# The work between the stages of a graph network kernel: loads, factors, a spill tile and a norm put elsewhere

## The chip, the cores and the metric

The kernel runs on one core of a Trainium2 chip. A core has TensorE (PE, matmuls), VectorE (DVE), ScalarE (ACT), GpSimd (POOL) and SyncE (SP, which only issues DMAs here). They run their own instruction streams and meet at semaphores. The metric is the device time of one execution in microseconds.

## The reference

12,500 nodes with 64 features, and 412,500 edges (200,000 random pairs in both directions and a loop for each node), sorted by destination. Three attention layers, then a mean-like graph convolution, each with a residual and a layer norm:

```python
x = features; out = features
for l in range(3):
    f1 = relu(x[row] @ nb_W[l] + nb_b[l]);  f2 = relu(x[col] @ self_W[l] + self_b[l])
    h = relu(concat([f1, f2]) @ att1_W[l] + att1_b[l])
    mask = clip(sigmoid(h @ att2_W[l] + att2_b[l]) * 1.5 - 0.45, 0, 1)
    d = clip((segment_sum(mask, row) + 1e-6) ** -0.5, 0, 10)
    x = segment_sum(mask * d[row] * d[col] * x[col], row)
    out = out + x
x = layernorm(features + out)
g = degree ** -0.5
h = relu(segment_sum(g[row] * g[col] * x[col], row) @ weight + bias)
return layernorm(x + h)
```

## The kernel before

**Blocks and tiles.** Nodes lie 128 to a block, in NB = 98 blocks of rows. The kernel first sorts the edges on chip and places those of a block of rows in TT = 50 tiles of 128 slots, in NG = 7 groups of 7 or 8 tiles (`GROUPS`, one PSUM bank each, `z_banks`). 49 tiles belong to pairs of column blocks; the 50th takes edges that did not fit, gathered by index (`xg`). What fits nowhere goes to "slow" spill tiles; with these inputs there is one of them (`n_slow` = 1), and `over_slow` loops over it. One-hot matrices for a block of rows (`oct`, `ort`, `orr`; 2.4 MB) are made in layer 0, kept in DRAM (`one_hots`) and loaded again in every later stage, in three pieces (`PIECES`).

**Stages.** Each of the layers 0 to 2 has a node stage (`node_stage`, `nodes_of`: two 64-wide products for each node, tables `q_table` and `p_planes` in DRAM), a score stage (`edges_of`: `cols` and `rows` matmuls, `hidden` and `logits` on DVE, a sigmoid on ACT, `masks`, `row_sums` into `rs`), a node factor `dinv` from `rs`, a scaled table (`scaled_table`: x times `dinv`, cut into three bf16 planes `tab` by `planes_of`, and stored as `xd_table` for the gathers) and a stage of sums (`segment_sums`). After layer 2 come a norm, a fourth scaled table and a fourth stage of sums with all masks 1, a last product and the last norm.

**A block in the stage of sums.** `cols` on PE picks the table rows of the 7 groups into PSUM. For each group DVE multiplies by the mask (`weighted`, L1828), ACT writes the high bf16 part back to PSUM (L908), DVE subtracts it (`rest`, L1835), POOL subtracts the next part (`low_planes`, L740), and PE adds all parts up by destination (`scatter`, L1180). DVE's order is `weighted` 0, `weighted` 1, `rest` 0, `weighted` 2, `rest` 1, and so on, with `sums` of the block before (L1840) behind `weighted` 3. POOL's order is the gather of the 50th tile (L670), groups 0 to 3, that tile's product (L728), groups 4 to 6. `z_ps`, `z_used`, `high_ps`, `low_ready`, `sc_ps` count these hand-overs. `over_rows` writes block 0 out and loops over the other 97.

**Between the stages.** SP issues in program order: the spill tile's loads, the store of the spill mask and a wait for it, a wait for all rows of the table, the table store (L623, 3136 KB in one DMA), then the one-hot loads of the stage (L500). POOL starts the stage when the store has landed. After the sums DVE adds the spill tile to `x_cur` (L1868), multiplies `x_cur` by `dinv` (L1901), and copies the next layer's weights (L1445, L1446), for which PE, ACT and POOL wait. POOL adds `x_cur` to `total` in the next score stage (L719). After layer 2 DVE adds it (L1913), and the norm is a row of passes over all 6272 columns: L1918 sum, L1922 subtract, L1924 square, L1926 sum, L1934 multiply; then the factor of the convolution, a memset of all masks (L1946), and the table.

Of the kernel before, what the change touches and what calls it, by code (L numbers as in the profile page):

```python
# [50 lines left out]
def gnn_kernel(nc, x, src, dst, nb_W, nb_b, self_W, self_b, att1_W, att1_b, att2_W, att2_b,  # L51
# [35 lines left out]
    TURNS_LATE = 12  # L87
    ROUNDS = -(-(E // S + NB) // XP)
# [15 lines left out]
    with ExitStack() as ctx:  # L104
# [255 lines left out]
        s_out = sem("slow_out")  # L360
        out_ready = sem("out_ready")
# [72 lines left out]
        def _(sp):  # L434
            sp.sem_inc(xd_out, 16)
# [104 lines left out]
            def edge_loads(layer):  # L540
# [22 lines left out]
                over_rows(sp, layer * (2 * NB), layer * NB, block_of_rows)  # L563
                rows_again(sp.snap(layer * NB + NB - 1), NB - 1)

            def segment_loads(t0, layer):
                def block_of_rows(t, m, R, late):
                    if not late:
                        wait_alone(sp, z_ps, t * NG + NG)
                        wait_alone(sp, sc_ps, m * NG + NG)  # L570
                        for i in range(3):
                            load_oct(R, i)
                        if not (isinstance(layer, int) and layer == L):
                            wait_alone(sp, rs_ps, layer * NB + NB + 1)
                        load_or(R, 0)
                        return
# [18 lines left out]
            def slow_loads(layer, first, edges):  # L595
                def tile(q, at, b):
# [8 lines left out]
                    if edges:  # L605
                        sp.dma_start(s_ix[:, 1, :], fields(sprow_d)).then_inc(s_in, 16)
                        wait_alone(sp, s_v, q * SLOW_V + 1 + SLOW_MASK)
                        sp.dma_start(smask_d[row, :].rearrange("o (p j) -> (o p) j", j=XS), s_mask).then_inc(s_out, 16)
                        wait_alone(sp, s_out, layer * n_slow * 16 + at * 16 + 16)
                    else:  # L610
                        sp.dma_start(s_mask, smask_d[row, :].rearrange("o (p j) -> (o p) j", j=XS)).then_inc(s_in, 16)
                over_slow(sp, n_slow, first, tile)

            def layer(l, first):
# [4 lines left out]
                else:  # L619
                    edge_loads(l)  # L620
# [1372 lines left out]
```

## Time and profile before

| | |
|---|---|
| median of 3 runs | 9728.46 us (9728.18 to 9734.29) |
| profiled execution | 9734.98 us, its span 9733.3 us |
| DVE, PE busy | 7868.9 us, 7865.2 us (81% each) |
| POOL, ACT busy | 3627.5 us, 3111.2 us |
| score stage of layer 1 | 4156 to 5326 us |
| sums of layer 0, 1, 2 | 3131 to 4050, 5378 to 6302, 7633 to 8555 us |
| sums of the convolution | 8654 to 9575 us |

The profile times every instruction of one execution, in microseconds from the span's start. The busy time of an engine is a share over stages that have different limits, so it is read stage by stage. Where an operation follows another of its engine at once, the two overlap a little, and the distance of the starts is what one costs.

### The profile page before, as it was taken

To read this page: it belongs to the slowest core of one execution; us is meant where nothing else is said; L and a number is where in the kernel's file an instruction comes from. 1 tells how busy PE (TensorE), PEld (TensorE's weight loads), DVE (VectorE), ACT (ScalarE), POOL (GpSimd) and SP (SyncE) were. 2 spreads that over 40 slices of the span, in tenths; PEclk is the share of its full clock that TensorE was granted. 3 is DMA by queue.
4 is the path that set the end of the run, shared out by engine and by line. 5 is a ranking of instruction groups with operands and counts; after the bars stand their busy time and mean duration, and the time that the engine had idled before them with its cause. 6 is when DMAs were issued, how large, how long until landed. Compare 5 with 4: busy or idle time off the path is not lost. (4 is left out here: it accounts for less than half of the span.)

```text
span 9733.3 us, 754656 instructions
## 1 busy us (share of the span) xinstructions
PE 7865.2 (81%) x306604; PEld 7523.1 (77%) x306604; DVE 7868.9 (81%) x13926; ACT 3111.2 (32%) x6110; POOL 3627.5 (37%) x4194
## 2 busy tenths in 40 slices
PE   0112239999997999989998899989999799959996
PEld 0012138888886999888997899879989799959995
DVE  9998169999997888877777788877777788878885
ACT  0010026666665444410001344320000344424442
POOL 0001510000001888510000788710000588848882
PEclk9755568999898999999999999999999899979996
DMA  1000137777775666567776666567777566646662
GB/s 28 0 0 11 33 94 241 240 240 239 241 241 179 178 178 178 141 198 209 206 208 179 170 179 178 155 174 207 209 207 207 152 178 177 178 113 178 178 177 71
DMA packets 983353, 1593.44 MB, mean 164 GB/s; under 512 B 249463, under 2 KB 732603, under 8 KB 982879
## 3 DMA queue, kind: packets, MB, share of 16 engines
q1 hardware_dynamic: 954104, 1563.61, 55.0%
q0 software_dynamic: 29152, 28.55, 1.7%
q8 instruction: 60, 0.98, 0.0%
q14 instruction: 37, 0.30, 0.0%
HBM read 1308.71 MB, written 283.01 MB: 164 GB/s over the span
## 5 line engine op out<-in xcount | busy, mean ns | idle before, releaser
L1053 PE MATMUL bank<-tab,extra 128*64 128x64 bf16 x201684 | 3599.9, 197 | 469.3 <-DMA extra<-one_hots 229.7
L1053 PEld LDWEIGHTS bank<-tab,extra 128*64 128x64 fp8e4 x201684 | 3478.8, 113 | 582.7 <-issue 555.7
L740 POOL TENSOR_TENSOR planes<-planes 128x448 f32<-128x448 f32 (+1 forms) x2744 | 2598.4, 950 | 540.0 <-DVE planes L1835 471.5
L908 ACT CAST bank<-planes 128x448 f32<-128x448 bf16 (+1 forms) x2744 | 1471.7, 545 | 1848.9 <-DVE planes L1828 1848.9
L1828 DVE TENSOR_TENSOR planes<-bank,mask_all 128x448 f32<-128x448 f32 (+2 forms) x2744 | 1665.9, 619 | 331.1 <-PE bank L1053 247.7
L1835 DVE TENSOR_TENSOR planes<-planes,bank 128x448 f32<-128x448 f32 (+1 forms) x2744 | 1707.6, 622 | 220.3 <-ACT bank L908 125.6
L1180 PE MATMUL bank<-planes,extra 128*64 128x192 bf16 x39200 | 1840.5, 248 | 16.5 <-issue 4.3
L1180 PEld LDWEIGHTS bank<-planes,extra 128*64 128x64 fp8e4 x39200 | 1685.6, 108 | 61.4 <-issue 11.1
L670 POOL DMA_INDIRECT xg<-q_table,ixb x294 | 279.0, 949 | 3761.2 <-ACT ixb L838 2204.7
L1708 DVE SCALAR_TENSOR_TENSOR extra<-bank,a2w 128x448 f32<-128x448 f32 (+1 forms) x2058 | 1263.6, 629 | 449.6 <-PE bank L1076 412.3
L1076 PE MATMUL bank<-plb,extra 128*128 128x64 bf16 x44100 | 1520.5, 196 | 10.7 <-issue 3.1
L1076 PEld LDWEIGHTS bank<-plb,extra 128*128 128x128 fp8e4 x44100 | 1424.0, 100 | 22.5 <-issue 10.3
L1715 DVE TENSOR_REDUCE lg<-extra 128x7 f32<-128x448 f32 (+1 forms) x2058 | 1232.4, 619 | 0.0
L869 ACT CAST extra<-bank 128x512 fp8e4<-128x512 f32 (+2 forms) x1470 | 717.3, 516 | 483.4 <-PE bank L1088 467.7
L1724 DVE TENSOR_SCALAR extra<-work,iota_p 128x2816 fp8e4<-128x2816 uint8 (+2 forms) x490 | 644.2, 1349 | 63.9 <-issue 30.6
L873 ACT COPY plb<-planes 128x192 bf16 (+1 forms) x294 | 103.8, 353 | 1607.0 <-PE bank L1076 1605.4
L970 PE MATMUL bank<-ident,tab 128*128 128x128 f32 x224 | 40.6, 366 | 676.1 <-DVE tab L1335 676.1
L970 PEld LDWEIGHTS bank<-ident,tab 128*128 128x128 f32 x224 | 39.0, 198 | 678.2 <-issue 344.2
L1088 PE MATMUL bank<-total,extra 128*128 128x128 bf16 x4900 | 511.5, 238 | 61.9 <-DVE rs L1696 42.7
L670 POOL DMA_INDIRECT xg<-xd_table,ixb x392 | 385.0, 982 | 315.4 <-issue 175.9
L1101 PE MATMUL bank<-mk,extra 128*128 128x4 bf16 x14700 | 410.3, 164 | 25.9 <-DVE mk L1692 14.4
L1101 PEld LDWEIGHTS bank<-mk,extra 128*128 128x128 fp8e4 x14700 | 392.1, 95 | 46.3 <-issue 33.9
(245 smaller groups left out, 4283.8 us busy)
## 6 DMA issues: line engine op xcount, KB each, us to landing
extra<-one_hots SPq DMA_DIRECT2D x1372, 352.0 KB, 3.1
extra<-one_hots SPq DMA_DIRECT2D x2156, 224.0 KB
extra<-one_hots SPq DMA_DIRECT2D x588, 208.0 KB
one_hots<-extra SPq DMA_DIRECT2D x490, 224.0 KB, 4.7
one_hots<-extra SPq DMA_DIRECT2D x294, 352.0 KB, 3.2
work<-slot_rows_cols SPq DMA_DIRECT2D x196, 352.0 KB, 4.9
work<-slot_rows_cols SPq DMA_DIRECT2D x294, 224.0 KB, 4.9
work<-slot_rows_cols SPq DMA_DIRECT2D x98, 208.0 KB
```

The lines of the kernel that those rows point to most:

```text
L670: nc.gpsimd.indirect_dma_start(out=to, out_offset=None, in_=table_d, in_offset=bass.IndirectOffsetOnAxis(ap=index, axis=0)).then_inc(done, 16)
L740: nc.gpsimd.tensor_tensor(tiles(yrl[:, 2, a * C:b * C]), tiles(yrl[:, 1, a * C:b * C]), upper[:, 1, a:b, :], ALU.subtract).then_inc(low_re ...
L869: nc.scalar.copy(orr[:, k * P:(k + n) * P], turn_to(j)[:, 0:n * P], saturate=False).then_inc(or_made, 1)
L908: nc.scalar.copy(tiles(z_banks[g][:, 0:(b - a) * C]), upper[:, 0, a:b, :]).then_inc(high_ps, 1)
L1053: mm = pe.matmul(bank[half * S:(half + 1) * S, i * C:(i + 1) * C], oct_[:, k * P + half * S:k * P + (half + 1) * S], tab[:, at:at + C], st ...
L1076: mm = pe.matmul(bank[:, i * C:(i + 1) * C], ort[:, k * P:(k + 1) * P], plb[:, pl * C:(pl + 1) * C], start=False, stop=True, skip_group_ch ...
L1101: mm = pe.matmul(sum_bank[:, 0:NPL + 1], orr[:, k * P:(k + 1) * P], mk_upper[:, k, :], start=(k == 0), stop=(k == TT - 1), skip_group_chec ...
L1180: mm = pe.matmul(sum_bank[lo:lo + S, 0:NPL * C], orr[:, k * P + lo:k * P + lo + S], upper[:, :, k, :], start=(k == 0), stop=(k == TT - 1))
L1708: v.scalar_tensor_tensor(tiles(yv[g % 3][:, 0:w]), tiles(bank_of(g, first)[:, 0:w]), 0.0, a2w[:].unsqueeze(1).to_broadcast([P, w // C, C]) ...
L1715: v.tensor_reduce(lg[:, k0:k1], tiles(yv[g % 3][:, 0:(k1 - k0) * C]), AX_X, ALU.add).then_inc(lg_done, 1)
L1828: v.tensor_tensor(tiles(yrl[:, 0, a * C:at * C]), tiles(z_banks[g][:, 0:(at - a) * C]), mask_all[:, bass.ds(R * TT + a, at - a)].unsqueeze ...
L1835: v.tensor_tensor(yrl[:, 1, a * C:b * C], yrl[:, 0, a * C:b * C], z_banks[g][:, 0:(b - a) * C], ALU.subtract).then_inc(z_used, 1)
```

## The change

1. `first_segment_loads`: SP issues the one-hot loads of the stage of sums ahead of the table store, which goes out in 7 parts (`scaled_rows_out`), each when its rows are scaled. `xd_out` counts the parts.
2. `scale`: the factor `dinv` and the addition to `total` are applied to the block before, in each turn of `segment_sums` of layers 0 to 2, behind `weighted` 5 and ahead of `rest` 4. The product over all of `x_cur`, POOL's additions to `total` and the last one on DVE are gone. The spill tile is added with its factor to both.
3. In layers 1 and 2 the spill tile of the score stage is worked on first on DVE and POOL, and behind block 0 on PE, ACT and SP (`behind_first`). Its matmul goes to `sum_bank`, `rs` begins as zeros, and `sums` adds to it. ACT issues the store of its mask.
4. The next layer's weights are copied behind block 0 of the sums, and ACT's sigmoid table is loaded there.
5. The norm after layer 2: no separate pass for squares on DVE (ACT squares parts while DVE subtracts and sums in turns), the two factors are joined into one for the table, POOL writes the normed x and the masks of ones.

```diff
-        def over_rows(eng, t0, n0, body):
+        def over_rows(eng, t0, n0, body, behind_first=None):
             body(value(eng, t0), value(eng, n0), 0, False)
+            if behind_first is not None:
+                behind_first()
...
+            def first_segment_loads(t0, layer):
+                wait_alone(sp, z_ps, value(sp, t0 * NG + NG))
+                wait_alone(sp, sc_ps, value(sp, layer * NB * NG + NG))
+                for i in range(3):
+                    load_oct(0, i)
+                if not (isinstance(layer, int) and layer == L):
+                    wait_alone(sp, rs_ps, value(sp, layer * NB + NB + 1))
+                load_or(0, 0)
+
+            def scaled_rows_out(k):
+                for i, (a, b) in enumerate(PARTS):
+                    wait_alone(sp, rows_ready, value(sp, k * NG + i + 1))
+                    sp.dma_start(table(xd_d)[:, a // C:b // C, :], w3[:, a // C:b // C, :]).then_inc(xd_out, 16)
...
-                        wait_alone(sp, s_v, q * SLOW_V + 1 + SLOW_MASK)
-                        sp.dma_start(smask_d[row, :].rearrange("o (p j) -> (o p) j", j=XS), s_mask).then_inc(s_out, 16)
-                        wait_alone(sp, s_out, layer * n_slow * 16 + at * 16 + 16)
...
-                slow_loads(l, l * 2, True)
-                wait_alone(sp, rows_ready, l * (2 * NG) + 2 * NG)
-                sp.dma_start(table(xd_d), w3).then_inc(xd_out, 16)
+                    edge_loads(l, lambda: slow_loads(l, l * 2, True))
...
+                first_segment_loads(l * (2 * NB) + NB, l)
+                scaled_rows_out(l * 2 + 1)
                 segment_loads(l * (2 * NB) + NB, l)
...
-                    if not late and not first:
-                        nc.gpsimd.tensor_tensor(total[:], total[:], x_cur[:], ALU.add).then_inc(total_added, 1)
...
+            wait_alone(pool, x_done, L * NB)
+            nc.gpsimd.memset(mask_all[:], 1.0).then_inc(ones_masks, 1)
+            pool.wait_ge(ones_masks, 1)
+            pool.wait_ge(norm_ready, 1)
+            for a, b in PARTS:
+                nc.gpsimd.tensor_tensor(x_cur[:, a:b].rearrange(view, c=C), total[:, a:b].rearrange(view, c=C),
+                                        nodeA[:, a // C:b // C].unsqueeze(2).to_broadcast([P, (b - a) // C, C]),
+                                        ALU.mult).then_inc(x_normed, 1)
...
+            def sigmoid_table(l):
+                wait_alone(act, layer_w, value(act, l + 1))
+                nc.scalar.activation(warm[:], a2b[:], ACT.Sigmoid)
...
+            for i, (a, b) in enumerate(PARTS):
+                wait_alone(act, centered, i + 1)
+                nc.scalar.activation(x_cur[:, a:b], total[:, a:b], ACT.Square).then_inc(part_squared, 1)
...
+                    edges_of(l, first, lambda: slow_edges(l, sum_bank))
...
+                def scale(t, R):
+
+                    rows, factor = bass.ds(value(dve, R * C), C), dinv[:, bass.ds(R, 1)]
+                    wait_alone(dve, or_done, t + 2)
+                    v.scalar_tensor_tensor(total[:, rows], to[:, rows], factor, total[:, rows], ALU.mult, ALU.add)
+                    v.tensor_scalar(to[:, rows], to[:, rows], factor, None, ALU.mult).then_inc(x_done, 1)
+
                 def block_of_rows(t, m, R, late):
                     for g in range(NG):
                         weighted(t, m, R, g)
                         if g == 3 and late:
                             sums(value(dve, m - 1), value(dve, R - 1))
+                        if g == 5 and late and scaled:
+                            scale(value(dve, t - 1), value(dve, R - 1))
                         if g:
                             rest(m, g - 1)
...
-                ns.done(v.tensor_tensor(x3, x3, per_node(dinv[:]), ALU.mult))
...
+            for i in range(NG + 2):
+                if i < NG:
+                    a, b = PARTS[i]
+                    rows = t3[:, a // C:b // C, :]
+                    v.tensor_tensor(rows, rows, dinv[:, a // C:b // C].unsqueeze(2).to_broadcast([P, (b - a) // C, C]),
+                                    ALU.subtract).then_inc(centered, 1)
+                if i >= 2:
+                    a, b = PARTS[i - 2]
+                    wait_alone(dve, part_squared, i - 1)
+                    ns.done(v.tensor_reduce(nodeA[:, a // C:b // C], x3[:, a // C:b // C, :], AX_X, ALU.add))
...
+            ns.done(v.tensor_tensor(g_both, nodeA[:], dinv[:], ALU.mult))
             ns.wait(dve)
-            scaled_table(2 * L)
-            segment_sums(L * 2 * NB, L, total)
+            scaled_table(2 * L, total, g_both)
+            dve.wait_ge(ones_masks, 1)
+            dve.wait_ge(x_normed, NG)
+            segment_sums(L * 2 * NB, L, total, False)
```

## Rows read from the trace of the kernel before

**Rows 1.** The page, busy us of each engine, share of the span, instructions.
```profile
PE 7865.2 (81%) x306604; PEld 7523.1 (77%) x306604; DVE 7868.9 (81%) x13926; ACT 3111.2 (32%) x6110; POOL 3627.5 (37%) x4194
```

**Rows 2.** Busy us in a stretch of layer 0's sums, PE clock, DMA share, GB/s.
```profile
3140.00:4035.00 895.00, 889.54 (x37800) 880.30 (x37795) 777.59 (x1436) 377.39 (x766) 747.71 (x860) 1.00 0.65 177
```

**Rows 3.** Waits in the same stretch: us in total, times, longest us.
```profile
DVE planes L1828 <- PE bank L1053: 39.9, 100, 2.3
```

**Rows 4.** Timeline of DVE in one block: start us, us, line, idle time before.
```profile
3605.13 0.61 DVE L1835 TENSOR_TENSOR planes<-planes,bank 128x448 f32<-128x448 f32 x1
3606.07 0.62 DVE L1828 TENSOR_TENSOR planes<-bank,mask_all 128x448 f32<-128x448 f32 x1 [0.33 <-PE bank L1053]
3606.62 0.35 DVE L1840 TENSOR_REDUCE x_cur<-bank 128x192 f32 x1
3606.88 0.61 DVE L1835 TENSOR_TENSOR planes<-planes,bank 128x448 f32<-128x448 f32 x1
...
3608.47 0.62 DVE L1828 TENSOR_TENSOR planes<-bank,mask_all 128x448 f32<-128x448 f32 x1
3609.01 0.61 DVE L1835 TENSOR_TENSOR planes<-planes,bank 128x448 f32<-128x448 f32 x1
```

**Rows 5.** Timeline of POOL in the same block.
```profile
3607.63 1.99 POOL L740 TENSOR_TENSOR planes<-planes 128x448 f32<-128x448 f32 x2 [0.81 <-DVE planes L1835]
3609.59 0.29 POOL L728 TENSOR_TENSOR planes<-xg,mask_all 128x64 f32<-128x64 f32 x1
```

**Rows 6.** Timeline of the first blocks of score stages 1 and 2.
```profile
4154.05 13.50 POOL L719 TENSOR_TENSOR total<-total,x_cur 128x6272 f32<-128x6272 f32 x1
...
4165.47 2.15 DVE L1685 TENSOR_SCALAR st_m<-sg 128x50 f32<-128x50 f32 x1 [0.55 <-ACT sg L843]
...
6408.32 13.48 POOL L719 TENSOR_TENSOR total<-total,x_cur 128x6272 f32<-128x6272 f32 x1
...
6419.99 1.86 DVE L1685 TENSOR_SCALAR st_m<-sg 128x50 f32<-128x50 f32 x1 [0.54 <-ACT sg L843]
```

**Rows 7.** Groups by line, DVE in the sort: count, busy us, mean ns.
```profile
L1335 DVE TENSOR_SCALAR tab<-tab,signs 128x4096 f32<-128x4096 f32 x7 | 16.5, 2353 | 0.3
```

**Rows 8.** Line L1685 in all layers: ns min, median, max.
```profile
L1685 DVE TENSOR_SCALAR st_m<-sg x294: 177/190/2149, 1412.7 to 7582.0; 128x50 f32<-128x50 f32 x147
```

**Rows 9.** Timeline where the sums of layer 0 and of the convolution start.
```profile
3111.31 0.39 SPq L623 DMA_DIRECT2D xd_table<-work  x1
...
3114.03 2.06 DVE L1435 TENSOR_TENSOR tab<-planes,tab 128x896 bf16<-128x896 f32 x2
...
3128.66 0.95 POOL L670 DMA_INDIRECT xg<-xd_table,ixb  x1 [44.14 <-DMA xd_table<-work]
...
3130.76 0.69 DVE L1828 TENSOR_TENSOR planes<-bank,mask_all 128x512 f32<-128x512 f32 x1 [14.68 <-PE bank L1053]
...
8653.72 0.69 DVE L1828 TENSOR_TENSOR planes<-bank,mask_all 128x512 f32<-128x512 f32 x1 [15.09 <-PE bank L1053]
```

**Rows 10.** Timeline between layer 0 and layer 1.
```profile
4055.32 0.22 DVE L1868 TENSOR_TENSOR x_cur<-x_cur,bank 128x64 f32 x1 [1.24 <-PE bank L1204]
...
4064.17 0.56 POOL L763 COPY extra<-x_cur 128x448 f32 x1 [12.48 <-DVE a2b L1446]
```

**Rows 11.** Timeline of the norm behind layer 2.
```profile
8560.22 0.22 DVE L1868 TENSOR_TENSOR x_cur<-x_cur,bank 128x64 f32 x1 [1.49 <-PE bank L1204]
...
8574.73 6.69 DVE L1918 TENSOR_REDUCE nodeA<-total 128x98 f32<-128x6272 f32 x1
...
8617.07 2.23 DVE L1677 TENSOR_TENSOR work<-x_cur,dinv 128x1024 f32<-128x1024 f32 x2
```

**Rows 12.** Timeline of DVE, first and last of score stage 1.
```profile
4156.76 1.42 DVE L1708 SCALAR_TENSOR_TENSOR extra<-bank,a2w 128x512 f32<-128x512 f32 x2 [3.76 <-PE bank L1076]
...
5332.25 0.16 DVE L1696 COPY rs<-bank 128x4 f32<-128x4 f32 x1 [4.44 <-PE bank L1101]
...
5337.87 0.46 DVE L1885 TENSOR_REDUCE dinv<-rs 128x98 f32<-128x294 f32 x1 [0.20 <-DVE rs L1816]
```

More of the change, by code:

```diff
@@ L568, in block_of_rows @@
                     if not late:
[L569 to L575, printed above, removed]
                         return
@@ L593, in segment_loads, with slow_loads @@
                     load_or(NB - 1, i)
-            def slow_loads(layer, first, edges):
+            def slow_loads(masks_of, first, edges):
                 def tile(q, at, b):
@@ L838, in indices, with sigmoids @@
                 nc.scalar.copy(ixb[:], colx[:, bass.ds(R * XT, XT)]).then_inc(ix_ready, 1)
-            def sigmoids(layer, first):
+            def sigmoids(layer, first, behind_first):
                 def sigmoid(n):
@@ L1056, in cols, with edges_of @@
                 return mm
-            def edges_of(layer, first):
+            def edges_of(layer, first, behind_first):
                 def cols_of(t, g):
@@ L1501, in _ @@
             layer_weights(0)
+            dve.wait_ge(layer_w, 1)
+            dve.wait_ge(xd_out, XD)
             nodes_of(0, True, range(0, 2))
@@ L1671, in _, with scaled_table @@
             dve.wait_ge(lo_out, LO_STORES * 16)
-            def scaled_table(k):
+            def scaled_table(k, rows, factor):
                 def scaled(i):
@@ L1815, in tile @@
                     at = rs[:, bass.ds(b, 1), :].rearrange("p o c -> p (o c)")
-                    sl.done(v.tensor_tensor(at, at, banks[0][:, 0:NPL + 1], ALU.add))
+                    sl.done(v.tensor_tensor(at, at, bank[:, 0:NPL + 1], ALU.add))
                     sl.wait(dve)
@@ L1819, in slow_edges, with segment_sums @@
                 over_slow(dve, n_slow, layer * 2, tile)
-            def segment_sums(t0, layer, to):
+            def segment_sums(t0, layer, to, scaled, behind_first=None):
                 def weighted(t, m, R, g):
@@ L1866, in tile @@
                     wait_alone(dve, s_p, q + 1)
-                    at = to[:, bass.ds(b * C, C)]
-                    sl.done(v.tensor_tensor(at, at, banks[0][:, 0:C], ALU.add))
+                    rows = bass.ds(b * C, C)
+                    if masked:
+                        for at in (total[:, rows], to[:, rows]):
+                            sl.done(v.scalar_tensor_tensor(at, banks[0][:, 0:C], dinv[:, bass.ds(b, 1)], at, ALU.mult, ALU.add))
+                    else:
+                        sl.done(v.tensor_tensor(to[:, rows], to[:, rows], banks[0][:, 0:C], ALU.add))
                     sl.wait(dve)
@@ L1876, in layer @@
                 if not first:
-                    layer_weights(l)
+                    ns.done(v.memset(rs[:], 0.0))
+                    ns.wait(dve)
+                    wait_alone(dve, layer_w, l + 1)
+                    wait_alone(dve, xd_out, l * XD + XD)
                     nodes_of(l, False, range(NCH // 2))
@@ L1881, in layer @@
                     planes_of(l * 2, "edges")
+                if not first:
+                    slow_edges(l, sum_bank)
                 edges_of(l, first)
-                slow_edges(l)
+                if first:
+                    slow_edges(l, banks[0])
                 ns.done(v.tensor_reduce(dinv[:], rs[:, :, 0:NPL], AX_X, ALU.add))
@@ L1911, in _ @@
             ns = Steps(nv, L * NODE_STEPS)
-            dve.wait_ge(total_added, L)
-            ns.done(v.tensor_tensor(total[:], total[:], x_cur[:], ALU.add))
-            ns.wait(dve)
-            dve.wait_ge(xd_out, L * 16 + 16)
+            dve.wait_ge(xd_out, (L + 1) * XD)
             def layer_norm(to3, z3, centered3, tmp3, r):
```

123 lines of the change are left out of this document (80 added, 43 removed).

## The prediction, made before the changed kernel was run

> **What bounds the kernel now.** I read the page first. The vector engine (DVE) and TensorE are both busy for about four fifths of the span [rows 1], which says only that no engine is idle enough to be ignored everywhere. The busy time by stretches says more. In the sums over segments of layer 0, TensorE works 889.5 of 895 us at the full clock of 2.4 GHz, DVE 777.6 and POOL 747.7 [rows 2]. There are four such stages of 98 blocks, so what a block gains or loses there counts 98 times per stage. TensorE bounds them, and the others are close behind.
>
> How close is read in one block. DVE's operations over 448 columns start 0.53 us apart although each lasts 0.61 to 0.62, so the cost of an operation in a row is the distance between starts. The fourth `weighted` stands at 3606.07, where 3605.66 (3605.13 plus 0.53) would have been possible: it waited for TensorE's columns [rows 4]. Over the stage this wait is 39.9 us in 100 times [rows 3]. With the 0.08 us by which two operations overlap, DVE has a slack of 0.5 us a block, and no other DVE start of the block waits for TensorE. All other gaps of the block are DVE's own length or an answer of ScalarE, and they move along with DVE. **If more than 0.5 us is added to DVE's block, the stage becomes DVE's.**
>
> Between the stages, little runs. At the change to the sums of layer 0, DVE finishes the table at about 3116.1. The table store was issued at 3111.31, POOL gets its rows at 3128.66, the one-hot loads queued behind the store release TensorE then too, and DVE's first `weighted` starts at 3130.76 after 14.7 us of idling; in the last of the four stages it is 15.1 us [rows 9], and the two between are alike.
>
> **The change part by part.**
>
> *Loads ahead of the store, store in parts.* Piece 0 of the store can leave when its rows are scaled, some 15 us before the last rows; the last part, a seventh of the 17 us that the store takes (2.4 us), and its latency end near 3116, just when the planes are ready. The one-hots are loaded long before. DVE's first `weighted` then follows the last plane: saving four times 14.7 to 15.1, 59 us. On SP the loads are moved in front of the store and nothing DVE needs is behind them; the spill tile's index loads stand before them. I allow 2 us a stage either way for how TensorE gets under way.
>
> *Node factor block by block.* At a layer's end the last spill sum ends at 4055.54 and POOL's first copy of the node stage starts at 4064.17 [rows 10]. Between lie a product over 6272 columns and six copies of weights. Afterwards about 1.1 us is left (a second small operation, semaphores, POOL's start): 7.5 us saved, twice, 15 us. The third time is in the next part.
>
> *Norm split up.* From 8560.44 to the table at 8617.07 it is 56.6 us [rows 11]: seven passes over 6272 columns of 6.69 us (46.8), the rest a memset and small steps. Left are one whole sum (6.7), seven subtractions and seven sums in turns (13.6), and some 4.3 us of roots, reciprocals and small steps: 24.6, so 32 us saved. The squares go to ScalarE, which is idle and covers a part in less than the 1.9 us between. POOL gets the ones (free, it is early) and a product of 6272 columns, which today takes it 13.5 us [rows 6] and lies beside 20 us of table making on DVE. If it hides, it costs nothing; if the two exclude each other, 13.5. I take 7.
>
> *Spill tile first, in layers 1 and 2.* The end gets shorter by the steps between the last row sum and the factor: 5332.25 to 5337.87 [rows 12], 5.2 us after a new wait. At the start DVE cannot touch `hidden` before the tile's sum, and the tile's matmuls stand behind TensorE's first block. So `hidden` begins at 4163 to 4165 in place of 4156.76 [rows 12]. TensorE then finds its banks late in block 1, but that block is late by loads and by POOL's long sum today, so I count 2 to 3 us. Net 5 us saved in all. In layer 0 the store of the mask leaves SP's queue; DVE's chain there is unchanged, 0.
>
> *Behind the first block.* Six weight copies on DVE beside a working POOL (2 us a stage, from 0.7 us of copies up to one POOL operation of 0.93 each for two of them) and ScalarE's table load: 6 us. Longer ends of the three stages: 1.5.
>
> Sum without the block-wise factor: -59 - 15 - 32 - 5 + 6 + 1.5 = -103.5, with POOL's product -96.5.
>
> *The factor's price.* Each of 98 blocks in three stages gets two DVE operations over 64 columns between the sixth `weighted` and `rest` of group 4, 294 pairs. By starts an operation of 192 columns takes 0.26 us [rows 4], one of 64 about 0.13: 0.26 a block, inside the slack of 0.5. That is the lower end, and it costs 0. But the second is a `tensor_scalar` from SBUF to SBUF in f32, the kind that does 4096 columns in 2353 ns [rows 7], 0.57 ns a column where the passes over 6272 columns take 1.07. This kind is held up by POOL: on the sigmoids it usually takes 0.19 us [rows 8], but once each in layers 1 and 2 it lasts 2.15 and 1.86 us and ends at 4167.62 and 6421.85, while POOL's `tensor_tensor` ends at 4167.55 and 6421.80 [rows 6]. Operations with a PSUM input run freely beside it. In the block POOL's `tensor_tensor` of group 3 lasts until 3609.62, and the pair comes up at 3609.01; behind it POOL has the extra rows ready until 3609.88 without a gap [rows 5]. Nothing more can come between, since POOL's group 4 waits for the `rest` that stands behind the pair. So the pair costs 0.26 if nothing waits; 0.64 if only the second waits and DVE gets in first; 0.77 if both wait and get in at 3609.62; 0.9 to 1.03 if DVE gets in only when POOL's run of two is over. I take 1.0, since POOL's second starts 0.03 us before the first has ended, which leaves no gap in the rows to get into. The period becomes DVE's, longer by 1.0 - 0.5 = 0.5 us: 294 x 0.5 = 147 us. POOL, ScalarE and TensorE have room in the longer period.
>
> Here the Trainium skill speaks against the change. "SBUF — State Buffer", section "Who interferes with whom", says that DVE's two-port modes and POOL exclude each other for a whole instruction, and also that a DVE operation with two SBUF inputs excludes a reading POOL instruction. The first half agrees with the two long rows; for the second half the trace has no case. By the whole rule both operations of the pair wait, and so do DVE's table operations beside POOL's product.
>
> Total: -96.5 + 147 = +50. The sum is made in the profiled execution (9734.98 us, span 9733.3); its differences carry over to the median 9728.5, so **9779 us**, 0.5% slower.
>
> **The rivals.**
> - *No wait* (other side). The pair is short or finds POOL between instructions. It stays in the slack, and only the gains are left: -104, 9625. For it: the first small cost fits. Against: POOL's two instructions cover the pair's time in the block [rows 5], and the long operations waited [rows 6]. It decides below 0.83 us a block, where loss and gain cancel (96.5 / 294 = 0.33 over the slack).
> - *Only the second operation waits, and DVE is next*: 0.14 over the slack, +41, together -62, 9666.
> - *Both wait, DVE gets in at the first POOL end*: 0.27 over the slack, +79 - 96.5 = -17, 9711.
> - *More than the wait*: the pair has four computed addresses and a semaphore wait. If these add 0.25 us that nothing covers, the block loses 0.75: +220 - 96.5 = +124, 9852.
> - *The store in parts does not release the stage* (SP or the queue still sets the start): up to 59 us of the gain is gone; it shifts each case up and is in the last one's chance.
>
> **How the numbers follow.** Forecast 0.42, its own range 9750 to 9815; no wait 0.14; second only 0.10; first end 0.18; more than the wait 0.16. Range 9640 to 9850: it leaves out most of "no wait" and the worst part of the last. A measurement of this kernel tells 0.2% (19 us) from no change. Faster by more: 0.14 + 0.10 and 0.07 of the third, 0.31. Same: the rest of the third and the forecast's lower edge, 0.14. Slower: 0.55.
>
> **What would show it.** In the changed profile: `scalar_tensor_tensor` or `tensor_scalar` of 64 columns in the sums lasting 0.5 us or more and ending just after POOL's operation; block period 9.7 to 9.9 us in place of 9.3; the wait of `weighted` for TensorE gone in three stages but not in the fourth; DVE idling under 1 us at stage starts; 24 to 32 us between the last spill sum and the last table. The prediction is wrong if the pair's operations take 0.2 us each beside POOL, or if TensorE is still busy without gaps in the stages of layers 0 to 2.

## The result and the profile after

The changed kernel takes **9746.02 us** (median of 20 runs, 9738.39 to 9750.23), the kernel before 9727.33 in the same session (20 runs, 9720.07 to 9736.72). The ratio is **1.0019**, 95% interval [1.0012, 1.0026]: 18.7 us slower. Predicted were 9779 us, 50 us slower. The direction held, the size did not: it was nearly three times too large. The profiled execution has a span of 9744.4 us, 11.1 longer than before.

The page's row of engines and the same stretch of layer 0's sums:

```profile
PE 7960.7 (82%) x306604; PEld 7586.3 (78%) x306604; DVE 8065.9 (83%) x14532; ACT 3120.4 (32%) x6120; POOL 3644.2 (37%) x4200
```
```profile
3140.00:4035.00 895.00, 875.64 (x36049) 858.47 (x36044) 813.14 (x1556) 360.61 (x731) 721.14 (x824) 1.00 0.64 169
```

Against [rows 2], TensorE does 36049 matmuls in the 895 us in place of 37800, POOL's work falls from 747.71 us to 721.14, and DVE's rises from 777.59 to 813.14: the stage has gone over to DVE. DVE's waits in this stretch say the same:

```profile
DVE planes L1878 <- ACT bank L936: 60.8, 183, 0.4
DVE planes L1871 <- issue: 10.6, 46, 0.2
DVE planes L1871 <- PE bank L1215: 10.4, 45, 0.2
```

The wait of `weighted` for TensorE's columns, 39.9 us in [rows 3], is gone. One block on DVE (start, length, line, operation, idle time before), the counterpart of [rows 4]:

```profile
3610.00 0.61 DVE L1878 TENSOR_TENSOR planes<-planes,bank 128x448 f32<-128x448 f32 x1
3610.53 0.62 DVE L1871 TENSOR_TENSOR planes<-bank,mask_all 128x448 f32<-128x448 f32 x1
3611.06 0.71 DVE L1890 SCALAR_TENSOR_TENSOR total<-x_cur,dinv,total  x1
3611.70 0.30 DVE L1891 TENSOR_SCALAR x_cur<-x_cur,dinv  x1
3611.91 0.61 DVE L1878 TENSOR_TENSOR planes<-planes,bank 128x448 f32<-128x448 f32 x1
...
4076.92 0.28 DVE L1890 SCALAR_TENSOR_TENSOR total<-x_cur,dinv,total 128x64 f32<-128x64 f32 x1
4077.12 0.25 DVE L1891 TENSOR_SCALAR x_cur<-x_cur,dinv 128x64 f32<-128x64 f32 x1
```

and on POOL, the counterpart of [rows 5]:

```profile
3609.70 2.00 POOL L753 TENSOR_TENSOR planes<-planes 128x448 f32<-128x448 f32 x2 [0.39 <-DVE planes L1878]
3611.65 0.29 POOL L741 TENSOR_TENSOR planes<-xg,mask_all 128x64 f32<-128x64 f32 x1
3612.67 1.93 POOL L753 TENSOR_TENSOR planes<-planes 128x448 f32<-128x448 f32 x2 [0.72 <-DVE planes L1878]
```

The pair starts at 3611.06 and the next `rest` at 3611.91: 0.85 us. The first of the pair ends at 3611.77, just behind POOL's group 3 at 3611.70. The same two operations for the last block, at 4076.92, where POOL only gathers, take 0.28 and 0.25 us. So the pair does wait for POOL, and the first of it gets in where POOL's group 3 ends: POOL's extra rows, which run from 3611.65, have not kept it out. The second comes up at 3611.70, while they run, and ends at 3612.00, just behind their end at 3611.94. In 291 blocks of the three layers it ends 0.05 us behind them and takes 0.30 us in place of 0.25, which fits a short wait of its own.

There is an exception, once in layer 1 and once in layer 2 (block 15, where POOL had started its groups late and works through them without a gap):

```profile
5534.41 2.50 DVE L1890 SCALAR_TENSOR_TENSOR total<-x_cur,dinv,total  x1
```
```profile
5533.12 3.71 POOL L753 TENSOR_TENSOR planes<-planes 128x512 f32<-128x512 f32 x4
```

Here the first operation comes up in POOL's second group and ends only behind the fourth, so POOL's next group went ahead of it twice.

The start of the sums of layer 0, and of the convolution behind them, the counterpart of [rows 9] (SP's seven parts of the store leave from 3093.42 on, POOL's gather starts at 3113.75, DVE's last plane ends at 3113.68):

```profile
3093.42 15.85 SPq L587 DMA_DIRECT2D xd_table<-work  x7
```
```profile
3111.61 2.07 DVE L1473 TENSOR_TENSOR tab<-planes,tab 128x896 bf16<-128x896 f32 x2
3113.95 1.22 DVE L1871 TENSOR_TENSOR planes<-bank,mask_all 128x512 f32<-128x512 f32 x2 [0.27 <-DVE tab L1473]
```
```profile
3113.75 0.95 POOL L685 DMA_INDIRECT xg<-xd_table,ixb  x1 [31.88 <-DMA xd_table<-work]
...
8633.33 17.11 POOL L795 TENSOR_TENSOR x_cur<-total,nodeA 128x1024 f32<-128x1024 f32 x7 [24.03 <-DVEq L2029]
```
```profile
8633.64 5.23 DVE L1715 TENSOR_TENSOR work<-total,rs 128x1024 f32<-128x1024 f32 x2
8638.79 2.70 DVE L1470 TENSOR_TENSOR planes<-work,tab 128x1024 f32<-128x1024 f32 x1
...
8652.31 1.08 DVE L1473 TENSOR_TENSOR tab<-planes,tab 128x896 bf16<-128x896 f32 x1
```

DVE idled 14.68 us ahead of its first `weighted` before and 0.27 now. In the convolution it is different: while POOL makes the normed x until 8650.4, DVE's table operations over 896 and 1024 columns take 2.4 to 2.7 us each, and 1.08 behind it.

Where the time went, step by step in the two profiled executions. Each step is the time from one landmark on DVE (or POOL) to the next; the block distance is the median distance of the first `weighted` of blocks 6 to 93.

| step, us before → after | layer 0 | layer 1 | layer 2 | convolution |
|---|---|---|---|---|
| table's start → first `weighted` | 36.24 → 21.84 | 36.82 → 21.98 | 36.48 → 21.98 | 36.66 → 31.82 |
| first `weighted` → block 5 | 53.76 → 50.64 | 55.91 → 50.09 | 54.24 → 50.40 | 53.95 → 52.59 |
| block 5 → block 97 | 854.65 → 900.18 | 856.66 → 895.85 | 856.61 → 894.14 | 856.47 → 857.24 |
| block distance | 9.286 → 9.784 | 9.313 → 9.718 | 9.313 → 9.697 | 9.306 → 9.316 |
| block 97 → last `sums` | 11.18 → 11.68 | 11.24 → 11.58 | 11.24 → 11.59 | 11.24 → 11.30 |
| last `sums` → next stage's first work | 13.82 → 6.22 | 17.36 → 6.22 | 62.03 → 34.23 | |
| POOL's first copy → first `hidden` | | 92.59 → 101.98 | 91.36 → 103.05 | |
| first `hidden` → block 5 | | 63.14 → 59.80 | 63.67 → 59.32 | |
| last `hidden` → `dinv` | | 13.43 → 5.91 | 12.95 → 5.92 | |

The first two rows together give 62.7 us (with what POOL's product costs the convolution already taken off), the changes of layer 18.7, the norm 27.8, the spill tile 1.4 (its start costs 21.1, the faster first blocks and the shorter ends give 7.7 and 14.6, the rest of the stage gives 0.2). Blocks 5 to 97 of the three stages take 122.2 us longer, 0.44 a block.

### The profile page after: what moved, and what is told of

Same layout as the page of the kernel before. It is cut to its first block and busy times, and to the rows that moved or that the text cites. A ratio compares the mean times of both kernels' runs of the same rounds, so it can differ in the third digit from the quotient of the medians.

```text
span 9744.4 us, 756265 instructions
## 1 busy us (share of the span) xinstructions
PE 7960.7 (82%) x306604; PEld 7586.3 (78%) x306604; DVE 8065.9 (83%) x14532; ACT 3120.4 (32%) x6120; POOL 3644.2 (37%) x4200
## 5 line engine op out<-in xcount | busy, mean ns | idle before, releaser
L1088 PE MATMUL bank<-tab,extra 128*64 128x64 bf16 x201684 | 3691.9, 197 | 400.8 <-issue 150.3
L1088 PEld LDWEIGHTS bank<-tab,extra 128*64 128x64 fp8e4 x201684 | 3535.0, 113 | 549.4 <-issue 521.8
```

Of the source, the lines that this page charges most:

```text
L1088: mm = pe.matmul(bank[half * S:(half + 1) * S, i * C:(i + 1) * C], oct_[:, k * P + half * S:k * P + (half + 1) * S], tab[:, at:at + C], st ...
```

## The experiments

Nine kernels ran, each beside the kernel before on the same chip: the other parts without the pair, the pair alone, its first operation alone and the pair behind `rest` 5 on one chip; the second operation alone, the pair in a gap, the norm's product by block and the table stored whole on another; the spill tile last on a third. On the second chip the kernel before takes 9336.12 us. It was not profiled there, but with the pair in a gap the sums of layer 0 take 854.4 us from block 5 to 97, as long as in the kernel before here; the score stages are shorter. So times are compared as ratios, and steps of one stage between profiles.

**The other parts without the pair.**

```diff
-                        if g == 5 and late and scaled:
-                            scale(value(dve, t - 1), value(dve, R - 1))
...
                 slow_segments(l * 2 + 1, x_cur, True)
+                v.tensor_tensor(x3, x3, per_node(dinv[:]), ALU.mult).then_inc(x_done, 1)
...
+                    if not late and not first:
+                        nc.gpsimd.tensor_tensor(total[:], total[:], x_cur[:], ALU.add).then_inc(total_added, 1)
```

> The changed kernel with the node factor as before: one product over 6272 columns at each layer's end, the sum into the total whole on POOL in the next layer's first block (whole on DVE ahead of the norm); loads, store in parts, weight copies, spill tile first and split norm stay. Theory (the block-wise pair costs 0.44 us in each of 294 blocks, the other parts gain on their own): the block period of the three stages falls from 9.72-9.79 back to 9.31-9.32 us, 130 us less; given back are 7.5 us at each of two layer ends, 14 us ahead of the norm (product and sum, 6.7 us each) and 3 to 4 us in the first blocks of two layers: 9653 us, 0.992 of the kernel before. Rival (the moved loads and stores or the weight copies slow the stages, not the pair): the period stays above 9.6 and the time above 9740.

Measured: 9655.67 us, ratio 0.9933 [0.992, 0.9947]; the block distance is back at 9.292, 9.319 and 9.320 us. In the stretch of [rows 2]:

```profile
3140.00:4035.00 895.00, 885.05 (x37490) 875.36 (x37483) 777.26 (x1434) 375.20 (x761) 746.38 (x861) 1.00 0.64 175
```

DVE's work is that of before again, and TensorE does nearly its matmuls of before. The pair is what lengthens the stages.

**The pair without the other parts**, in the kernel before:

```diff
                         if g == 3 and late:
                             sums(value(dve, m - 1), value(dve, R - 1))
+                        if g == 5 and late and scaled:
+                            scale(value(dve, t - 1), value(dve, R - 1))
...
-                ns.done(v.tensor_tensor(x3, x3, per_node(dinv[:]), ALU.mult))
...
-                        nc.gpsimd.tensor_tensor(total[:], total[:], x_cur[:], ALU.add).then_inc(total_added, 1)
```

> The kernel before with the block-wise factor alone: scalar_tensor_tensor and tensor_scalar over 64 columns between the sixth weighted and the fourth rest, no whole product, no sum on POOL; all else as before. Theory (pair costs 0.44 us a block by itself): period 9.72-9.79 in three stages, +130; saved are 6.7 us at two layer ends, 13.4 us ahead of the norm and 3 to 4 us in the first blocks of two layers: about +96, 9823 us, 1.010. Rival (the stages are slowed by the other parts): period 9.31 and 9692 us, 0.996.

Measured: 9808.11 us, ratio 1.0088 [1.0074, 1.0102]. The block distance is 9.681, 9.680 and 9.679 us: 0.37 to 0.40 a block over before, with none of the other parts changed. In the kernel before, the fourth `weighted` starts 0.96 us behind the operation ahead of it in layer 0 and 1.03 in layers 1 and 2 (medians of blocks 6 to 93), where 0.53 would do: the slack is 0.43 and 0.50, and the pair's 0.85 less that is 0.42 and 0.35. The changed kernel has 0.02 to 0.10 more. In layer 0 this lies at `rest` 0, which waits for ScalarE and starts 0.96 us behind the second `weighted`, in place of 0.86 in this run; in layers 1 and 2 the next block's first `weighted` starts 0.88 and 0.84 us behind the last `rest`, in place of 0.79, and the trace names nothing that it waits for. Why the other parts do this stays open.

**The first of the pair alone.** This kernel leaves x without its factor.

```diff
-                    v.scalar_tensor_tensor(total[:, rows], to[:, rows], factor, total[:, rows], ALU.mult, ALU.add)
-                    v.tensor_scalar(to[:, rows], to[:, rows], factor, None, ALU.mult).then_inc(x_done, 1)
+                    v.scalar_tensor_tensor(total[:, rows], to[:, rows], factor, total[:, rows], ALU.mult, ALU.add).then_inc(x_done, 1)
```

> The changed kernel without the second operation of the pair (x of the segments is left unscaled: only the total gets the factor). Theory (the first operation, with two SBUF inputs, waits for the end of POOL's group 3; the second starts 0.22 us ahead of the next rest and adds just that): period 9.50 to 9.57 in place of 9.72 to 9.79, first operation still 0.7 us long; 0.22 x 294 = 65 us under the changed kernel, 9681. Rival (only the second waits): first operation 0.3 us long or less, period 9.31, 120 us less.

Measured: 9688.32 us, ratio 0.9963 [0.995, 0.9977], block distance 9.560, 9.536 and 9.530. The group of the operation in layer 0's sums (count, busy us, mean ns):

```profile
L1890 DVE SCALAR_TENSOR_TENSOR total<-x_cur,dinv,total x74 | 52.0, 703 | 0.0
```

It waits by itself, and the second one adds 0.17 to 0.22 us a block. The rival, with a first operation of 0.3 us, is out.

**The second of the pair alone.** This kernel leaves the stage's sums out of `total`.

```diff
-                    v.scalar_tensor_tensor(total[:, rows], to[:, rows], factor, total[:, rows], ALU.mult, ALU.add)
```

> The changed kernel without the first operation of the pair (the total gets no segment sums). Only the tensor_scalar with one SBUF input is left, coming up at 6.06 us of the block, where POOL's group 3 runs until 6.69 and its extra rows from 6.65 to 6.94. In the run with the pair behind rest 5 this operation came up 0.03 us behind the start of a POOL group and lasted 0.95 us, so it waits too. Theory A (a waiting DVE operation gets in where POOL's running instruction ends): 0.7 us long, period 9.5 to 9.57 as with the first operation alone, 9680 us, 0.9955. Theory B (this kind gets in only when POOL's run of two is over, at 6.94): 0.9 to 0.95 us long, period 9.70 to 9.78, within 15 us of the changed kernel. Rival (one SBUF input doesn't wait at this place): 0.2 us long, period 9.31, 9625 us.

Measured: ratio 0.9936 [0.9919, 0.9952] (9277.88 us beside 9336.12), block distance 9.547 in layer 0, and 9.479 and 9.420 in the next two, a little under the 9.5 expected and far from theory B's 9.70. A block on DVE and on POOL:

```profile
3503.58 0.62 DVE L1871 TENSOR_TENSOR planes<-bank,mask_all 128x448 f32<-128x448 f32 x1
3504.12 0.68 DVE L1890 TENSOR_SCALAR x_cur<-x_cur,dinv  x1
3504.72 0.61 DVE L1878 TENSOR_TENSOR planes<-planes,bank 128x448 f32<-128x448 f32 x1
```
```profile
3502.75 2.00 POOL L753 TENSOR_TENSOR planes<-planes 128x448 f32<-128x448 f32 x2 [0.40 <-DVE planes L1878]
3504.70 0.29 POOL L741 TENSOR_TENSOR planes<-xg,mask_all 128x64 f32<-128x64 f32 x1
```

It comes up at 3504.12, ends at 3504.80, 0.05 behind POOL's group 3 (3504.75), and POOL's extra rows, which run from 3504.70 to 3504.99, have not kept it out. So it goes in 288 of the 294 blocks; in four, the last of each layer among them, it meets no end of POOL, and in two (block 15 of layers 1 and 2) it stands for 2.5 us, through three ends. Theory A holds for this place: a waiting DVE operation gets in at the end of POOL's running instruction, where the prediction took the end of POOL's whole run. It is no rule without exception, and what makes POOL's groups go first in block 15 stays open.

**The pair at another place**, behind `rest` 5, where DVE idles 0.3 us.

```diff
-                        if g == 5 and late and scaled:
-                            scale(value(dve, t - 1), value(dve, R - 1))
...
                             rest(m, g - 1)
+                    if late and scaled:
+                        scale(value(dve, t - 1), value(dve, R - 1))
                     rest(m, NG - 1)
```

> The changed kernel with the pair moved behind the rest of group 5, where DVE idles 0.3 us for ScalarE before the last rest. Theory (the price is the wait for POOL's running instruction, and it depends on the place): the pair's first operation comes up while POOL's group 4 has 0.2 us or less left, and it goes in front of group 5; delay of the last rest 0.3 us or less, under the slack of 0.5: period 9.31 to 9.35, 120 to 130 us less than the changed kernel, 9620, 0.989. Rival (the price is the pair's own: addresses, the semaphore wait, two starts): 0.85 us less the idle 0.3, period 9.35 to 9.45, and both operations 0.3 us or less. Second rival (POOL's groups are pushed back and TensorE waits for them): period above 9.6 and DVE waiting for y or TensorE.

Measured: 9698.79 us, ratio 0.9977 [0.9967, 0.9986], block distance 9.588 to 9.606. It is faster than the changed kernel, but 80 us short of what was expected. DVE and POOL in one block:

```profile
5608.96 0.61 DVE L1878 TENSOR_TENSOR planes<-planes,bank 128x448 f32<-128x448 f32 x1
5609.49 0.32 DVE L1890 SCALAR_TENSOR_TENSOR total<-x_cur,dinv,total  x1
5609.74 0.96 DVE L1891 TENSOR_SCALAR x_cur<-x_cur,dinv  x1
5610.61 0.61 DVE L1878 TENSOR_TENSOR planes<-planes,bank 128x448 f32<-128x448 f32 x1
```
```profile
5608.55 0.29 POOL L741 TENSOR_TENSOR planes<-xg,mask_all 128x64 f32<-128x64 f32 x1
5608.80 1.85 POOL L753 TENSOR_TENSOR planes<-planes 128x448 f32<-128x448 f32 x2
```

The first gets in at the end of POOL's group 4, as expected. But the second comes up at 5609.74, a few hundredths of a microsecond after POOL's group 5 has begun (two groups in 1.85 us, so the second starts near 5609.7), and it stands until 5610.70, when that one is over (5610.65). Each of two waiting operations needs an end of its own. In the changed kernel the second end came 0.25 us behind the first, with the short extra rows; here it comes a whole group later. The expectation counted one wait for the pair. This is not the whole of the miss: the fourth `weighted` still waits for TensorE here (23.3 us in 82 times in 800 us of layer 1's sums), as the second rival said, so how the loss divides between the two isn't shown.

**The pair in a gap of both engines**: in the next block but one, behind `weighted` 1, where DVE idles for ScalarE and POOL issues a gather.

```diff
                 def block_of_rows(t, m, R, late, third=False):
...
-                        if g == 5 and late and scaled:
-                            scale(value(dve, t - 1), value(dve, R - 1))
+                        if g == 1 and third:
+                            scale(value(dve, t - 2), value(dve, R - 2))
```

> The changed kernel with the pair moved into the next block but one, behind the second weighted, where DVE idles 0.25 us for ScalarE and POOL only issues a gather (no operation on data until the first rest is done). Theory (the price is the wait for POOL's instructions): both operations 0.3 us or less, 0 to 0.1 us of delay of the first rest, inside the slack; period 9.31 to 9.34, minus 125 us against the changed kernel: 9620, 0.989. Rival (0.25 us or more of own cost of issue, addresses and the semaphore wait): period 9.31 still but the first five blocks and tails longer by some us. Second rival (the pair and POOL's gather exclude each other): operations of 0.7 us or more, or a gather over 1.1 us, and period above 9.5.

Measured: ratio **0.9883** [0.9866, 0.9899] (9226.96 us beside 9336.12, 109 us less), block distance 9.280, 9.317 and 9.319: that of before. DVE and POOL:

```profile
5500.37 1.22 DVE L1871 TENSOR_TENSOR planes<-bank,mask_all 128x512 f32<-128x512 f32 x2 [0.30 <-issue]
5501.51 0.28 DVE L1890 SCALAR_TENSOR_TENSOR total<-x_cur,dinv,total  x1
5501.70 0.25 DVE L1891 TENSOR_SCALAR x_cur<-x_cur,dinv  x1
5501.86 0.68 DVE L1878 TENSOR_TENSOR planes<-planes,bank 128x512 f32<-128x512 f32 x1
...
5503.91 0.62 DVE L1871 TENSOR_TENSOR planes<-bank,mask_all 128x448 f32<-128x448 f32 x1 [0.30 <-PE bank L1088]
```
```profile
5501.35 0.98 POOL L685 DMA_INDIRECT xg<-xd_table,ixb  x1 [0.20 <-issue]
5502.69 1.99 POOL L753 TENSOR_TENSOR planes<-planes 128x512 f32<-128x512 f32 x2 [0.36 <-DVE planes L1878]
```

Same two operations, same addresses, same semaphore wait: 0.35 us from the first to the next `rest` in place of 0.85, the gather still 0.98, and TensorE sets the block again (the 0.30 at `weighted` 3 is its wait). So 0.50 of the 0.85 was the wait for POOL, and the 0.35 of the pair's own lies inside the slack. The second rival is out, since the gather and the pair kept their lengths. Of the first nothing is seen: the first five blocks take 48.8 to 49.2 us, as in the kernel without the pair (48.8 to 49.3).

**The norm's product in the blocks of the last stage** besides.

```diff
-            for a, b in PARTS:
-                nc.gpsimd.tensor_tensor(x_cur[:, a:b].rearrange(view, c=C), total[:, a:b].rearrange(view, c=C),
...
+                    if normed:
+                        rows = bass.ds(value(pool, R * C), C)
+                        nc.gpsimd.tensor_tensor(x_cur[:, rows], total[:, rows], nodeA[:, bass.ds(value(pool, R), 1)].to_broadcast([P, C]),
+                                                ALU.mult).then_inc(x_normed, 1)
```

> As the pair in the gap, and POOL's product of the norm over 6272 columns made in the last stage's blocks instead, 64 columns at the start of each block (tensor_tensor with a broadcast factor). Theory (DVE's table operations wait for POOL's product): from the table's start to the first weighted 21.9 us in place of 31.8; the 98 small POOL operations of some 0.15 us find POOL idle 0.2 us or more before its gather, so the last stage's period stays 9.31: 10 us under the pair in the gap, 9610, 0.988. Rival (the small POOL operations hold up DVE's first weighted or delay the gather): last stage's period 9.4 or more, which costs 9 us per 0.1 us and eats the gain.

Measured: ratio **0.9868** [0.9852, 0.9884] (9213.62 us), the fastest of the versions, 13 us under the one before. From the table's start to the first `weighted` of the convolution it takes 21.84 us in place of 31.83, and the block distance there is 9.312. So POOL's product cost the changed kernel 10.0 us.

**The table stored whole**, with the loads still ahead.

```diff
-                for i, (a, b) in enumerate(PARTS):
-                    wait_alone(sp, rows_ready, value(sp, k * NG + i + 1))
-                    sp.dma_start(table(xd_d)[:, a // C:b // C, :], w3[:, a // C:b // C, :]).then_inc(xd_out, 16)
+                wait_alone(sp, rows_ready, value(sp, k * NG + NG))
+                sp.dma_start(table(xd_d), w3).then_inc(xd_out, 16)
```

> The changed kernel with the scaled table stored whole when its last rows are scaled, the one-hot loads still ahead of it. Theory (the loads ahead give the first half of the stage starts' gain and the faster first blocks, the store in parts gives the time until the table has landed): the store is issued where it was before (2.8 us ahead of the first plane operations' last, some 17 us long), POOL's rows for the first block come 10 to 15 us later, but POOL is needed only at group 0 of the extra rows: DVE's first weighted starts at once, 22 us behind the table's start, and the block's last group waits; first five blocks 8 to 12 us longer in four stages, +30 to +50 us, 9785. Rival (loads alone release the stage, the table lands in time): within 10 us of the changed kernel.

Measured: ratio 1.0062 [1.0045, 1.0079] (9393.95 us beside 9336.12), which is 0.43% or 40 us over the changed kernel's ratio. DVE in the first block of layer 0's sums, and the store and POOL's answer to it:

```profile
2882.38 1.22 DVE L1870 TENSOR_TENSOR planes<-bank,mask_all 128x512 f32<-128x512 f32 x2 [0.27 <-DVE tab L1472]
...
2889.18 0.61 DVE L1877 TENSOR_TENSOR planes<-planes,bank 128x448 f32<-128x448 f32 x1
2900.39 0.62 DVE L1877 TENSOR_TENSOR planes<-planes,bank 128x448 f32<-128x448 f32 x1 [10.61 <-ACT bank L935]
```
```profile
2877.33 0.39 SPq L586 DMA_DIRECT2D xd_table<-work  x1
```
```profile
2894.74 0.95 POOL L684 DMA_INDIRECT xg<-xd_table,ixb  x1 [44.52 <-DMA xd_table<-work]
```

DVE starts at once, since the loads are ahead, and the wait for the table appears at the end of the block. From the table's start to block 5 it takes 90.0 us before, 84.3 so and 72.5 in the changed kernel: the loads ahead give 5.7 and the store in parts 11.8.

**The spill tile last again**, on top of the best version.

```diff
-                    edge_loads(l, lambda: slow_loads(l, l * 2, True))
-                if first:
-                    slow_loads(l, l * 2, True)
+                    edge_loads(l, None)
+                slow_loads(l, l * 2, True)
...
-                    slow_edges(l, sum_bank)
                 edges_of(l, first)
-                if first:
-                    slow_edges(l, banks[0])
+                slow_edges(l, banks[0])
```

> As the run with the pair in the gap and the norm's product by block, but in the score stages of layers 1 and 2 the spill tile comes behind the rows again, as before. Theory (as predicted: the tile costs nearly as much in front as it saves behind): from the last hidden operation to dinv 13 us in place of 5.9 (+14 in two layers); from POOL's copy of the node stage to the fifth block of hidden operations 10 to 14 us less in each of two layers, since DVE no longer waits for the tile's gathers: -7 net, or 0.1% faster than with the tile in front. Rival (the predicted 5 us gain): 5 us longer. Either is inside the interval of the times, so the steps of the profiles decide.

Measured: 9609.19 us, ratio 0.9883 [0.9867, 0.99], within the intervals the same as with the tile in front. By the steps, against the changed kernel, whose score stages are as long on that chip: POOL's first copy to the first `hidden` 92.04 and 93.62 us (9.9 and 9.4 less), to the fifth block 3.7 and 2.8 more, the rest of the stage 2.0 and 1.5 less, the end 7.7 and 7.3 more. That is 0.7 and 0.8 us less: neither the 7 expected nor the 5 predicted the other way; the order of the tile is worth under 2 us. Its last stage took 7.6 us longer, at a distance of 9.392 a block with DVE still waiting for TensorE; this is one profile, and its cause stays open.

## Why the prediction came out as it did

It named the right mechanism (the pair waits for POOL and the stage becomes DVE's) and the right side, and a total that was 31 us too high by the medians (+50 against +18.7) and 39 by the profiled executions (+11.1), in which its sum was made; 9746 us lies just under the forecast's own range of 9750 to 9815. The steps, in its own terms and the profiled executions' time:

- **The pair: predicted 1.0 us a block, measured 0.85.** This is the step that failed: "I take 1.0, since POOL's second starts 0.03 us before the first has ended, which leaves no gap in the rows to get into." DVE needs no gap. The second operation alone ended 0.05 us behind POOL's group 3 with POOL's next instruction already there. As a pair, each takes an end of its own: the first that of group 3 (0.63 us from its start to the second's), the second that of the extra rows, and as its own length is covered by the wait it adds 0.22. The rival "gets in at the first POOL end" was right about the first operation, and with 0.77 a little low, since the second waits again.
- **What that does to a block: predicted 0.5 for a pair of 1.0, measured 0.44 for one of 0.85.** With the slack of 0.5, 0.85 would have added 0.35, 103 us. Over blocks 5 to 97 the changed kernel lost 122.2 us, which is 130 for 294 pairs, against 147. So the price was 44 us too high, and 27 us of that were hidden by what the sum left out: in layer 0 the slack is 0.43 (the 39.9 us of [rows 3] hold a few long waits), `rest` 0 there waits 0.10 longer for ScalarE, the next block starts 0.06 and 0.02 later in layers 1 and 2, and in block 15 of both the pair stands for 2.5 us. That these cancel in part is luck.
- **The side was near the edge.** By the prediction's own sum the pair breaks even at 0.83 us. At the measured 0.85 it gives -96.5 + 103 = +6 us, which could not be told from no change.
- **Stage starts: predicted 59, less 7 for POOL's product beside the last of them; measured 62.7 with the product in it.** The run that took the product away gives 10.0 for it, so the starts alone are 72.7. Of the two bounds for the product, 0 and 13.5, the upper was nearer. The starts gave more than the four times 14.7 to 15.1 of idle time, because the first five blocks, whose one-hots are now loaded early, are 3.1 to 5.8 us shorter too in layers 0 to 2 and 1.4 in the convolution, which the prediction left out but for 2 us either way.
- **Between layers: predicted 15, measured 18.7.** In layer 1 the last `sums` stood 17.36 us from POOL's copy before, in layer 0 13.82; only the latter had been read [rows 10].
- **The norm: predicted 32, measured 27.8.** Of the difference, 2.3 us lie ahead of the last spill sum, which starts 7.5 us behind the last `sums` in place of 5.2: DVE waits longer for the spill tile's gather, and SP now issues the next stage's loads just ahead of it (8599.40, the gather at 8599.83); whether that is the cause isn't shown. Another 1.3 are a `tensor_scalar` over 98 columns that takes 1.57 us beside POOL's memset of the masks, which was called free; in the kernel without the pair, where the memset is over by then, it takes 0.25.
- **The spill tile: predicted 5, measured 1.4**, and nothing by the run that undid it. Its wait in front is longer than read: `hidden` starts 9.4 us later after POOL's copy in layer 1 and 11.7 in layer 2, where 6 to 8 had been read.
- **Behind the first block: predicted 6 lost; longer ends: 1.5.** The first can't be told apart, since the first five blocks got shorter by 14.1 in all. The ends took 1.2.

So the gains were 109 us in place of 96.5, and the pair cost 122 (its part in the first five blocks is in the stage starts) in place of 147: 13 and 25 us, which make up 38 of the 39. The case "no wait" had been priced at -104 us; with the pair in the gap it measured -109, on another chip. The signs named for the changed profile appeared: the pair's first operation over 0.5 us, a distance of 9.7 to 9.8, TensorE's wait gone in three stages and not in the fourth, and DVE idling under 1 us at the starts. Between the starts of the last spill sum and the last table lie 26.7 us (8606.95 to 8633.64).

"SBUF — State Buffer" of the Trainium skill, section "Who interferes with whom", had been weighed against the trace, with the half on two SBUF inputs unproven. The runs agree with both halves: the `scalar_tensor_tensor` with two SBUF inputs takes 0.28 us alone and 0.71 beside POOL's `tensor_tensor`, the `tensor_scalar` 0.25 and 0.68.

## What to carry to other kernels

An operation moved into a busy loop costs what it meets there, not what it takes alone: the same pair, 0.53 us by its two lengths, took 0.85 beside POOL, 1.12 us (5609.49 to 5610.61) at a place that was idle on DVE only, and 0.35 in a gap of both engines. Look at both engines' rows at the very place, and let a result wait a block longer if the gap is there. A pair that is cheap by itself can eat a hundred microseconds of real gains, so run the parts of such a change one by one.

## What the runs showed of the hardware

- A DVE operation that waits for POOL mostly gets in at the end of POOL's running instruction, even when POOL's next one stands ready (3504.70 against 3504.75 above): so in 288 of 294 blocks for the `tensor_scalar` alone, and in 289 for the `scalar_tensor_tensor` alone. In two blocks of each of these kernels POOL's next two groups went first, and the operation took 2.5 us.
- Two such operations in a row take two ends: the second lasted 0.96 us in the median of 294 when POOL's next group began 0.02 us before it, and 0.30 when it was the short extra rows.
- Waiting covers most of a DVE operation's own time: the `scalar_tensor_tensor` that takes 0.28 us alone ended 0.08 us behind POOL's instruction, the `tensor_scalar` of 0.25 alone 0.05 (medians).
- Over long operations the exclusion works both ways: POOL's product over 6272 columns took 17.11 us beside DVE's table, where POOL's sum over as many takes 13.5 [rows 6] (its first part of 1024 columns, begun ahead of DVE, took 1.96 us, the five of 896 columns 2.53 to 2.66); DVE's 896 columns took 2.57 us in place of 1.08. A gather of POOL (0.98 us) and the pair did not hold each other up.
- A memset of POOL, which reads nothing, held up a `tensor_scalar`: POOL's memset ran from 8605.02 to 8609.31, the operation from 8607.80 to 8609.37, 1.57 us in place of 0.25 in the kernel without the pair.

```profile
8605.02 4.29 POOL L791 MEMSET mask_all<- 128x4900 f32 x1 [4.24 <-DMA extra<-xd_table,s_fld]
```
```profile
8607.80 1.57 DVE L1999 TENSOR_SCALAR nodeA<-rs 128x98 f32<-128x98 f32 x1 [0.58 <-DVEq L1929]
```

- Chips differ: the kernel before took 9722.61 and 9719.61 us on two and 9336.12 on a third. There the score stage of layer 1 takes 1030 us from block 5 to the last in the kernel with the pair in a gap, in place of 1104 to 1105 in the kernels before and after here; the stages of sums take the same. In 900 us of that stage TensorE is busy 884 us in place of the 839 of the kernel before here, and the core moves 222 GB/s in place of 207, at the full granted clock (2.4 GHz) in both. What makes the chips differ isn't shown.
